# A four-stage graph network on one core: nine semaphore waits of TensorE's queue dropped, so that it has 1024 instructions a graph

## The reference

```python
h = jnp.maximum(_layernorm(x, axis=-1), 0.0)
x = x + _L0_gnn_ref(h, adj, ...)   # 2 layers: softmax(h h^T) * adj; upper part @ hl + diagonal * hs + lower part @ hr; layer norm
...
x = x + _L1_gnn_ref(h, adj, ...)   # 2 layers: u from h and two weighted h, exp, * adj, @ h_lin; layer norm
...
x = x + _L2_gnn_ref(h, adj, ...)   # 12 heads, scores + 2 adj, softmax, @ v, @ Wo
...
x = x + _L3_gnn_ref(h, adj, ...)   # 12 heads, scores masked by adj, softmax, @ v
```

## Time and profile before

| what | value |
|---|---|
| median of 3 runs | 2867.77 us (2862.84 to 2868.46) |
| profiled execution, its own time | 2869.98 us |
| its span, first to last instruction | 2868.3 us |
| granted TensorE clock | 0.999 of full speed |
| PE busy | 2762.5 us (96%) |
| DVE busy | 2437.3 us (85%) |
| ACT busy | 2115.4 us (74%) |
| POOL busy | 847.0 us (30%) |

### The profile page before, as it was taken

One profiled execution on the slowest core, in us unless ns is written; L12 is line 12 of the kernel. 1 busy time (PEld: TensorE's weight loads), 2 busy tenths in 40 slices (PEclk: granted clock), 3 DMA queues, 4 the chain that ended last, 5 costly groups with the idle time before them and its releaser, 6 DMA issues.

```text
span 2868.3 us, 87271 instructions
## 1 busy us (share of the span) xinstructions
PE 2762.5 (96%) x33523; PEld 2095.5 (73%) x33523; DVE 2437.3 (85%) x7450; ACT 2115.4 (74%) x6036; POOL 847.0 (30%) x1227
## 2 busy tenths in 40 slices
PE   8999999999999999999999999999999999999998
PEld 6777777777777777777777777777777777777787
DVE  5888898898898888888898898898898888888884
ACT  6777777777777777777777777777777777777763
POOL 1233233233233233233233233233233232332321
PEclk9999999999999999999999999999999999999999
DMA  6233333333332233232343333343332332333332
GB/s 205 55 66 58 56 66 55 58 66 56 58 68 58 53 66 58 53 68 53 58 68 53 59 67 52 61 68 51 60 68 51 60 66 51 63 59 53 63 59 42
DMA packets 560621, 180.01 MB, mean 63 GB/s; under 512 B 517712, under 2 KB 560208, under 8 KB 560208
## 3 DMA queue, kind: packets, MB, share of 16 engines
q1 hardware_dynamic: 560208, 174.43, 33.0%
HBM read 35.92 MB, written 12.58 MB: 17 GB/s over the span
## 4 chain that ended last, share of the span: by engine, by line
PE 70%; DMA 8%; DVE 8%; ACT 6%; issue 4%; POOL 2%; SPq 1%; ACTq 0%; DVEq 0%; POOLq 0%
PE bank_c L387 22%; PE bank_a L387 18%; PE bank_b L387 14%; DMA pt_halves<-prob_halves 6%; PE bank_c L556 4%; PE bank_b L419 3%; DVE score L1078 3%; PE bank_c L433 3%; POOL prob_halves L1234 2%; DVE neg_head_max L1083 2%; PE bank_b L426 1%; ACT node_b L659 1%; SPq L317 1%; DVE prob_halves L1093 1%; ACT node_b_halves L731 1%
## 5 line engine op out<-in xcount | busy, mean ns | idle before, releaser
L1234 POOL TENSOR_TENSOR prob_halves<-prob,prob_halves 128x384 f16<-128x384 f32 x512 | 471.0, 925 | 944.8 <-DVE prob_halves L1093 944.8
L795 ACT ACTIVATE prob<-score,neg_head_max 128x128 f32<-128x128 f32 x1536 | 495.6, 392 | 90.1 <-DVE neg_head_max L1083 89.0
L387 PE MATMUL bank_c<-htc_hi,w_hi 128*128 128x128 f16 x2304 | 399.0, 219 | 0.0
L387 PE MATMUL bank_c<-htc_lo,w_hi 128*128 128x128 f16 x2304 | 399.0, 219 | 0.0
L387 PE MATMUL bank_c<-htc_hi,w_lo 128*128 128x128 f16 x2304 | 399.0, 219 | 0.0
L387 PE MATMUL bank_a<-w_hi,hta_hi 128*128 128x384 f16 x1152 | 375.8, 327 | 21.9 <-ACT bank_a L654 21.4
L387 PE MATMUL bank_a<-w_lo,hta_hi 128*128 128x384 f16 x1152 | 375.3, 326 | 0.0
L1078 DVE SCALAR_TENSOR_TENSOR score<-bank_c,bias 128x384 f32<-128x384 f32 x512 | 281.3, 549 | 82.1 <-PE bank_c L556 78.6
L654 ACT ACTIVATE m_hi<-bank_b 128x384 f16<-128x384 f32 x256 | 124.3, 486 | 227.6 <-PE bank_b L426 140.4
L1083 DVE TENSOR_REDUCE neg_head_max<-score 128x3 f32<-128x384 f32 x512 | 280.8, 548 | 6.7
L387 PE MATMUL bank_a<-w_hi,hta_lo 128*128 128x384 f16 x1152 | 250.5, 327 | 0.0
(11 more groups left out here) (194 smaller groups left out, 8461.9 us busy)
## 6 DMA issues: line engine op xcount, KB each, us to landing
x_in<-x SPq DMA_DIRECT2D x64, 192.0 KB, 2.4
out<-y_out SPq DMA_DIRECT2D x64, 192.0 KB, 2.2
pt_halves<-prob_halves SPq DMA_TRANSPOSE x512, 2.8
w_stage<-w_t SPq DMA_DIRECT2D x11, 576.0 KB, 5.8
adj_in<-adj SPq DMA_DIRECT2D x64, 64.0 KB, 1.8
adj_t<-adj_turned SPq DMA_DIRECT2D x64, 64.0 KB, 2.1
score<-w_t SPq DMA_DIRECT2D x4, 576.0 KB, 7.8
prob<-w_t SPq DMA_DIRECT2D x4, 576.0 KB, 5.3
```

Of the source, the lines that this page charges most:

```text
L387: mm = nc.tensor.matmul(out_ap, a, b, start=first and i == 0, stop=last and i == len(pairs_of) - 1, skip_group_check=True)
L795: ex = nc.scalar.activation(prob[:, j, c, :], score[:, j, c, :], ACT.Exp, bias=neg_head_max[:, j, c:c + 1])
L1234: P.tensor_tensor(prob_halves[:, j, 1, :, :], prob[:, j, :, :], prob_halves[:, j, 0, :, :], ALU.subtract)\
```

## The change

Nine waits of PE per graph are dropped: attn_a_ready ahead of L470 (two layers), hta_lo_ready and hl_ready in `weight_a` (two layers each), mr_ready in `weight_b` (two layers) and attn_tb_ready of the graph before in `weight_b` (first layer). Each of them is implied by another wait that stays. For the last this holds because SP's wait ahead of the DMA that writes htb is changed from ub_done to attn_tb_ready. No product, no copy and no DMA is added, removed or moved, and the idle products stay.

```diff
@@ SP, turn_nodes_b
                     if k == 1 and g:
                         sp.wait_ge(*lin_done.at(g - 1, 2))
-                        sp.wait_ge(*ub_done.at(g - 1, 2))
+                        sp.wait_ge(*attn_tb_ready.at(g - 1, 2))
@@ PE, chain_a
-                    pe.wait_ge(*attn_a_ready.at(g, k))
                     pe.wait_ge(*self_ready.at(g, k))
                     nc.tensor.transpose(a0[:, 0:128], attn_a[:, :], ident[:, :]).then_inc(ata_done[g], 1)
@@ PE, weight_a
                     weights(g, l, 0)
-                    pe.wait_ge(*hta_lo_ready.at(g, k))
                     pe.wait_ge(*bias_a_set.at(g, 3 * l + 1))
...
-                    pe.wait_ge(*hl_ready.at(g, k))
                     weights(g, l, 2)
                     pe.wait_ge(*bias_a_set.at(g, 3 * l + 3))
@@ PE, weight_b
                     pe.wait_ge(*htb_landed.at(g, k))
-                    if l == 0 and g:
-                        pe.wait_ge(*attn_tb_ready.at(g - 1, 2))
                     for o in range(CHUNKS):
...
-                    pe.wait_ge(*mr_ready.at(g, k))
                     weights(g, 2 + l, 2)
                     pe.wait_ge(*bias_b_set.at(g, k))
```

## The result

The changed kernel takes 2892.25 us, median of 4 runs (2889.24 to 2895.0). The kernel before, run beside it, takes 2868.11 us (2862.84 to 2870.13). The two medians are 24 us apart. The ratio as it was taken is 1.0072, 95% interval 1.0053 to 1.0092: slower by 0.7%, which is 21 us. 2898 us had been predicted. The profiled execution took 2889.8 us with a span of 2888.0, so it is 19.7 us longer in span than the one of before.

What follows compares the result with a forecast made beforehand. PE, busy 96%, was taken as the bound, its code packets lengthening transposes it needs. 2870.0 + 30.6 - 0 = 2900.6, less 2.2 for the median, gave 2898 us; likeliest range 2885 to 2912, wider 2859 to 2913.

Steps and rivals of the forecast that it cites:

- The count: PE's instructions a graph fall from 1,033 to 1,024 = 4 x 256, so packet boundaries stand at one place for all graphs.
- the two packets fewer: Over the whole run, 576 instructions fewer at 256 a packet; expected to change the time by nothing.
- Which place: Mark (first L470 product of a graph) at 3 modulo 256 in every graph from the third on, resembling slow graph 28.
- Rival (a): Packet moves 2.4 us or more after the fourth layer 4 transpose's issue and misses it: -39 us, 2829 us; chance 0.12.
- The first term of the sum: Sixty graphs with packets at the slow place take 43.73 us each instead of 43.22: +30.6 us, bounds +17 and +44.
- The waits' own time: Dropped waits save 0.09 us where PE stands, third weight product of layer 1 and L470: 11 us at most, taken as 0.
- Rival (c): The code fetch is neutral and the 11 us of dropped waits are kept: 2857 us, faster; chance 0.05.
- SP's wait: The htb transpose's wait for attn_tb_ready in place of ub_done has 3.7 us of cover in every graph: cost 0.
- Marks 43.5 to 44 us apart in nearly all graphs: Expected sign in the profile after: L470 marks so spaced, with no return to 42.6 us for a run of graphs.
- PE's wait for pt_halves: Expected sign before L587: wait for the transposed probabilities near 60 x 1.1 = 65 us against 32.4.
- The wait before L470 still near 58 times: Expected sign: PE still waits there about as often, 0.09 us shorter each time.
- No new wait for htb: Expected sign: PE gets no new wait for the htb transpose in the profile after.

Runs made afterwards that it cites:

- e2: The changed kernel with 94 idle products ahead of the first step in place of 110 (mark at 227 modulo 256): 2929.0 us, ratio 1.0194.
- e10: The changed kernel with 80 idle products ahead of the first step in place of 110 (mark at 199 modulo 256): 2830.39 us, ratio 0.9852.
- e1: The changed kernel with 72 idle products ahead of the first step in place of 110 (mark at 183 modulo 256): 2830.89 us, ratio 0.9852.
- e4: The kernel before with only SP's edit: first htb transpose waits for attn_tb_ready in place of ub_done, PE keeps all waits; 2872.87 us, ratio 0.9994.
- e3: The changed kernel with nine separate waits a graph put in at other PE products, 1,033 instructions a graph again: 2860.56 us, ratio 0.9955.

## Why the prediction was right

**The count.** 1,024 = 4 x 256 fixes the place, as predicted. In the changed kernel each packet moves at one place of the graph, to within 1.5 us; the two packets fewer (266 against 268) are as counted. Moving the start by a number that is no multiple of 128 idle products can move the time by up to 98 us, while 128 brings it back. This is shown by the runs, and no other difference between these kernels is left.

**Which place.** The mark at 3 had to be slow through the fourth transpose of layer 4, and is: 4.2 us with one packet in its time, and 64 waits. Rival (a), that the packet misses the transpose, would have given 2829 us; the mark at 183 and at 199 is that rival, and gives 2831 and 2830. Its price was right and its place was not this one. The edge it named, 2.4 us after the issue, does not hold as an edge: e2 has slow transposes with the packet up to 2.8 us after the issue, and e10 quick ones from 2.4 on. The place counted in instructions sets the two apart, the packet's moment doesn't. That is one of the ways of being wrong that the prediction named, and the changed kernel, with its packet at about 2.0 us, was far enough from it.

**The mis-sized term.** The first term of the sum said 60 x (43.73 - 43.22) = +30.6 us; by the marks it is 60 x (43.57 - 43.22) = +21, and the sixty graphs took 20.9 more. The graph that resembles all graphs of after was taken as the mean over graphs 28, 29, 56 and 57, 43.73 us, which is 0.16 us too much. Four graphs can't give it more closely: in the changed kernel the sixty graphs, with their packets at the same places, scatter by 0.40 us (standard deviation), so that a mean of four is uncertain by 0.20 us, 12 us in the run. Graph 57 alone, 43.5 us and named as the lower bound with +17, is as near from the other side.

A difference between the four can be seen: graphs 28, 29 and 56 have their second packet at 21.5 to 22.1 us after the mark and graph 57 has it at 16.9, and in the changed kernel it is at 16.8 to 17.6 in all sixty graphs. But that doesn't explain the size: graph 30 of the kernel before has it at 16.7 and takes 43.77 us, with a fourth transpose of 4.6 us where graph 57 has 4.3. How long that transpose gets differs from graph to graph, 3.8 to 5.3 us in the changed kernel, and the graph's time goes with it. So the term was mis-sized within what a sample of four allows.

**The waits' own time.** It was set at 0 of at most 11 us. The mechanism can be seen. At the third weight product of layer 1 PE now starts 0.05 us after the release instead of 0.14 (the chain of the changed kernel: start, us, what):

```profile
1344.32 0.39 ACT bank_a L648
1344.71 0.05 issue
1344.76 0.82 PE bank_a L387 x4
```

Behind the four products the transpose of node_c waits, as before, but now its weight load stands 0.39 us instead of 0.33:

```profile
1344.83 0.71 ACT L653 ACTIVATE node_c<-x,shift_c,rstd_c 128x384 f32<-128x384 f32 x1
...
1345.59 0.20 PEld L433 LDWEIGHTS bank_c<-ident,node_c 128*128 128x128 f32 x2 [0.39 <-ACT node_c L653]
```

From the release to this weight load it is 1345.59 - 1344.71 = 0.88 us, and before it was 1422.22 - 1421.34 = 0.88. So the 0.09 us is passed on whole, as the prediction argued. At L470 two clean graphs show the same, graph 20 of the kernel before (its mark is at 862.99 us) and graph 28 of e1 (mark at 1195.55):

```profile
883.49 0.30 PE L470 MATMUL bank_a<-ident,attn_a 128*128 128x128 f32 x1 [0.40 <-ACT bank_a L722]
...
889.18 0.27 PE L387 MATMUL bank_b<-m_hi,htb 128*128 128x256 f16 x1
...
1215.96 0.33 PE L469 MATMUL bank_a<-ident,attn_a 128*128 128x128 f32 x1 [0.31 <-ACT bank_a L716]
...
1221.74 0.27 PE L387 MATMUL bank_b<-m_hi,htb 128*128 128x256 f16 x1
```

The transpose of attn_a comes 20.50 us after the mark before and 20.41 in e1; the product that needs m_lo comes after 26.19 us in both. (It is the second of the graph's two L470 products, so the wait is in the second layer, not in "layer 0"; no number hangs on that.)

The clean graphs of e1 bear it out in sum: the wait before L469 is 18.7 us in 60 (0.31 each, against 23.1 / 58 = 0.40 before) and that before the weight product 13.4 in 60 (0.22, against 21.4 / 63 = 0.34), yet a clean graph takes as long as before. Four such graphs of e1 in a row:

```profile
L469 PE MATMUL bank_a<-ident,attn_a x9: 278/279/328, 1153.0 to 1323.2; 128*128 128x128 f32 x9
```

To 0.01 us these marks are at 1152.99 and 1323.24, 42.56 us a graph without the nine waits; with them, from 820.41 to 948.15, it is 42.58. So about 1 of the 11 us was kept, and under 2. Rival (c) falls: the trace shows the time saved and where it goes.

**SP's wait** was set at 0; e4 has it at 0.9994 (0.9984 to 1.0005). The cover of 3.7 us is still there in the changed kernel: attn_tb_lo ends at 1343.04, node_b_halves at 1346.73, and the DMA is issued behind it.

```profile
1342.76 0.28 DVE L872 SCALAR_TENSOR_TENSOR attn_tb_lo<-bank_b,attn_tb_hi 128x128 f16<-128x128 f32 x1
...
1346.18 0.55 DVE L875 SCALAR_TENSOR_TENSOR node_b_halves<-node_b,node_b_halves 128x384 f16<-128x384 f32 x1
...
1346.76 1.21 SPq L328 DMA_TRANSPOSE htb<-node_b_halves  x1
```

**What did not come as said.** "Marks 43.5 to 44 us apart in nearly all graphs" was wrong: 29 of the sixty are below 43.5 us and 7 above 44, and only the mean of 43.57 falls into that range. PE's wait for pt_halves was put near 65 us and is 57.1. "The wait before L470 still near 58 times" was wrong: it is 26 times, 6.8 us. A PE that is held 0.7 to 1.3 us at the transpose arrives later at L469, when ACT is often done; so part of a stall is given back there: 18.7 - 6.8 = 12 us in the run, by e1, which has dropped the same waits and has no such stalls. "No new wait for htb" was wrong too. Each graph has two htb transposes, and in the changed kernel a packet meets both in all sixty graphs: the second packet, 0.7 us after the issue of the one, and the fourth packet, 2.4 us after the issue of the other. From issue to landing, in us (minimum, median, maximum), htb took 2.7, 2.8 and 5.0 before. In the changed kernel it takes, over the whole run and then for the two of graph 30, issued at 1324.15 and 1346.76 us,

```profile
DMA to landing us min/median/max: 2.8/4.0/4.8
...
DMA to landing us min/median/max: 3.6/3.6/3.6
...
DMA to landing us min/median/max: 4.5/4.5/4.5
```

PE waits 10.2 us for htb, against 7.7 before, and nearly all of it is for the first of the two; the second, though longer, lands in time. SP's edit is not the cause of that: in e1 and e10, which have the edit, the median is back at 2.8. The errors on L470 and htb are smaller than the term of the transposes and work against each other.

The page of the Trainium skill "Runtime: NRT & Kernel Launch", section "Instruction fetch mechanics", calls the cost of crossing a block of code "mostly hidden". The measurement decides against it for this kernel: 2830 or 2929 us by the place of the crossings alone, with one crossing more or less in all. The loss is not PE waiting for its code, though. It comes by way of a transpose; where the packets meet none that PE needs, as in e1, a graph takes 42.57 us with four of them.

## What to carry to other kernels

When graphs or tiles that run the same instructions take different times, look at the queue that moves an engine's own code, and at what else moves while a packet does. Count the instructions of one round of the loop modulo the packet: with a multiple, each round has the packets at one place, and dropping or adding a few instructions is then mostly a bet on that place. Once it is fixed, choose it by a few instructions ahead of the loop and time several choices, since the places of the packets in a trace don't follow the count closely enough to tell. Here the changed kernel with 72 or 80 idle products in place of 110 beats both kernels, 2830 us, while 94 makes it the slowest of all. An edit that takes out instructions should therefore be timed at more than one start, or its own worth (here under 2 us) can't be told from the place's (98 us).

## What the runs showed of the hardware

One packet of 16 KB of PE's code that moves 1.9 to 2.3 us after the issue of a transposing DMA makes it 4.1 to 4.6 us long in most graphs, up to 5.3, instead of 2.8; the packet's own time is about 1.0 us. That holds for the fourth and the first transpose of layer 4, for the first of layer 5 and for htb (4.5 us in graph 30 of the changed kernel). A packet 0.7 us after the issue costs less: 3.6 us, the other htb of that graph.

From 2.3 to 2.8 us after the issue both outcomes occur: slow in all graphs of e2, with packets of 1.0 us, quick in nearly all of e10, with packets of 1.2 to 1.9 us. Packets 2.9 to 4 us after the issue leave the transpose as it is in 84 of 88 graphs of the twelve kernels. That the place matters is shown by moving it; why the transpose is longer by more than the packet's own time stays open.

A separate wait instruction costs PE 0.09 us where PE stands and nothing that could be measured elsewhere: the nine other waits of e3 did not make the kernel slower.
